# A depthwise convolution on TensorE: the first convolution's matmuls cut from 32x64 to 32x32 array tiles

## The reference

```
h = x.transpose(0, 2, 1)
h = conv1d_grouped(h, conv1_w, conv1_b, c)     # 256 groups: 1 channel -> 4 hidden, 5 taps, padding 2
h = gelu(h)
h = conv1d_grouped(h, conv2_w, conv2_b, c)     # 256 groups: 4 hidden -> 1 channel, 5 taps
h = layernorm(h.transpose(0, 2, 1) + x, ln0_g, ln0_b)
```

## Time and profile before

| what | value |
|---|---|
| median of 3 runs | 1867.98 us (1865.91 to 1868.26) |
| the profiled execution | 1865.91 us |
| its span, first to last instruction | 1864.1 us |
| mean granted TensorE clock | 0.997 of full |
| busy: PE, PEld, DVE, ACT, POOL | 99%, 82%, 76%, 50%, 54% of the span |
| busy in 18.84 to 58.00 us: PE, DVE, ACT, POOL | 39.16, 20.01, 21.70, 11.85 of 39.16 us |
| the 32 steps of the convolutions | 5.7 us to 153.4 us |

### The profile page before, as it was taken

How to read it: one execution, slowest core, us unless ns; L and a number is a source line. 1 busy time by engine, 2 the same in 40 slices (tenths; PEclk the granted TensorE clock), 3 DMA queues, 4 the chain that set the end, 5 groups by cost and what they waited for, 6 DMA issues and landing times.

```text
span 1864.1 us, 47990 instructions
## 1 busy us (share of the span) xinstructions
PE 1837.3 (99%) x20164; PEld 1527.0 (82%) x20164; DVE 1417.9 (76%) x3329; ACT 933.9 (50%) x1741; POOL 1010.7 (54%) x775
## 2 busy tenths in 40 slices
PE   8999999999999999999999999999999999999998
PEld 2335888888888888888887899999999999999998
DVE  3667788888888888888887757777777777777777
ACT  4554766677666766677666742222222222323221
POOL 1557998999989998999884012121212122222221
PEclk9999999999999999999999999999999999999999
DMA  8273210000102210000106831010101010101000
GB/s 305 116 267 119 92 59 2 14 25 2 36 2 104 92 36 2 26 12 2 59 2 213 283 97 46 24 39 30 35 35 35 33 36 24 46 23 46 23 12 24
DMA packets 25240, 115.49 MB, mean 62 GB/s; under 512 B 4480, under 2 KB 5440, under 8 KB 19904
## 3 DMA queue, kind: packets, MB, share of 16 engines
q1 hardware_dynamic: 21104, 89.69, 13.7%
q0 software_dynamic: 1152, 12.58, 1.9%
q10 hardware_dynamic: 2768, 10.15, 1.4%
HBM read 80.95 MB, written 31.46 MB: 60 GB/s over the span
## 4 chain that ended last, share of the span: by engine, by line
PE 95%; DVE 2%; ACT 1%; POOL 1%; issue 1%; DMA 0%; SPq 0%; ACTq 0%; DVEq 0%; POOLq 0%
PE bankC L33 13%; PE bankC L34 13%; PE bankC L32 13%; PE ring L32 7%; PE ring L34 6%; PE ring L33 6%; PE big L917 5%; PE big L34 3%; PE big L33 3%; PE big L32 3%; PE ring L854 3%; PE big L834 3%; PE hid_ps L242 3%; PE conv_ps L253 3%; PE ring L891 2%; PE ring L876 2%
## 5 line engine op out<-in xcount | busy, mean ns | idle before, releaser
L32 PE MATMUL bankC<-down_hi,act_hi 128*128 128x256 f32 x1024 | 290.4, 284 | 0.0
L33 PE MATMUL bankC<-down_lo,act_hi 128*128 128x256 f32 x1024 | 290.0, 283 | 0.0
L34 PE MATMUL bankC<-down_hi,act_lo 128*128 128x256 f32 x1024 | 289.6, 283 | 0.0
L1553 DVE TENSOR_TENSOR act_lo<-gel,act_hi 128x512 fp32r<-128x512 f32 x256 | 210.5, 822 | 8.8
L32 PE MATMUL bankC<-aT_hi,up_hi 128*128 128x512 f32 x512 | 202.2, 395 | 0.0
L34 PE MATMUL bankC<-aT_hi,up_lo 128*128 128x512 f32 x512 | 202.2, 395 | 0.0
L33 PE MATMUL bankC<-aT_lo,up_hi 128*128 128x512 f32 x512 | 202.1, 395 | 0.0
L1507 POOL TENSOR_TENSOR hC<-hC,vecC 128x1024 f32<-128x1024 f32 x16 | 38.7, 2419 | 291.3 <-PE turn L1406 291.3
L32 PEld LDWEIGHTS bankC<-down_hi,act_hi 128*128 128x128 f32 x1024 | 193.5, 189 | 1.4
L33 PEld LDWEIGHTS bankC<-down_lo,act_hi 128*128 128x128 f32 x1024 | 192.6, 188 | 1.4
L1513 POOL TENSOR_TENSOR rstdC<-var_epsC,minus_halfC 128x4 f32<-128x4 f32 x47 | 52.5, 1118 | 260.1 <-DVE var_epsC L1578 260.1
(11 more groups left out here) (205 smaller groups left out, 5241.3 us busy)
## 6 DMA issues: line engine op xcount, KB each, us to landing
raw_late<-in_AB SPq DMA_DIRECT2D x30, 320.0 KB, 3.7
u<-hA SPq DMA_DIRECT2D x8, 1024.0 KB, 5.0
u_next<-u SPq DMA_DIRECT2D x8, 1024.0 KB, 4.8
hC<-u SPq DMA_DIRECT2D x16, 512.0 KB, 4.0
xC<-in_x SPq DMA_DIRECT2D x16, 512.0 KB, 4.9
out<-w_flat SPq DMA_DIRECT2D x15, 512.0 KB, 2.6
w_flat<-in_AB SPq DMA_DIRECT2D x22, 320.0 KB, 3.8
w_split<-w_parts ACTq DMA_DIRECT2D x4, 1536.0 KB, 5.1
```

The costliest lines, as they stand in the source:

```text
L32: e.matmul(out, wh, xh, start=start, stop=False)
L33: e.matmul(out, wh, xl, start=False, stop=False)
L34: return e.matmul(out, wl, xh, start=False, stop=stop)
L1553: e.tensor_tensor(a_lo[:, fb, :], g, a_hi[:, fb, :].bitcast(F32), ALU.subtract).then_inc(s_act_lo, 1)
```

## The change

In `conv1`, each matmul with a 32x64 stationary tile (two positions s) is replaced by two with 32x32 tiles (one position s each), so there are 32 calls per step instead of 16. The loop over `half` becomes a loop over s; the choice of k is the same for s = 0, 1 and for s = 2, 3 as it was for the two halves. For each output element the two products are added in the same order as before. The wait for a free bank stands ahead of each call as before (only the first for each bank has an effect), and the increment of `s_hid` sits on the last call of each bank.

```
-                    for half in range(2):
-                        k = 1 - second if half else second
+                    for s in range(S):
+                        k = second if s < 2 else 1 - second
                         for j in range(ROWS):
-                            r, rows = slice(32 * j, 32 * j + 32), slice(64 * half, 64 * half + 64)
-                            out = hid_of(n, j)[rows, :].rearrange("p (b g) -> p b g", b=2)
+                            r = slice(32 * j, 32 * j + 32)
+                            out = hid_of(n, j)[32 * s:32 * s + 32, :].rearrange("p (b g) -> p b g", b=2)
                             src = xs[l][r, cp, k:k + COLS].rearrange("p (b g) -> p b g", b=2)
-                            bands = band1[r, cp, k, 2 * half:2 * half + 2, :].rearrange("p s c -> p (s c)")
                             w.wait_ge(s_hidden, ROWS * n + j - HID + 1)
-                            m = e.matmul(out[:, :, second:], bands, src[:, :, second:], start=not second, stop=bool(second))
-                            if second and half:
+                            m = e.matmul(out[:, :, second:], band1[r, cp, k, s, :], src[:, :, second:], start=not second,
+                                         stop=bool(second))
+                            if second and s == S - 1:
                                 m.then_inc(s_hid, 1)
```

## The result

The changed kernel takes 1877.32 us (median of 6 runs, 1874.20 to 1878.01), the kernel before 1867.31 us (6 runs, 1864.01 to 1868.26). The ratio is 1.0055 with a 95% interval of 1.0043 to 1.0066: 10 us slower, where +1.0 us was forecast, a range of 1865.0 to 1874.0 us, and 0.76 on "within 0.2%". The profiled execution took 1879.74 us, its span is 1877.9 us.

A forecast was written before the change was run, and what follows sets the result against it. PE was taken to bound the convolution stage; -0.02 + 0.056 = +0.036 us per step over 31 steps gave +1.1 us, less 0.14 us swallowed by waits, net +1.0 us: 1869.0 us, range 1865.0 to 1874.0 us.

The forecast's parts named there:

- Streaming: In conv1, sixteen tiles run at once, so four waves of 0.43 us remain and streaming costs nothing more.
- column tiles take turns: Rival: in conv1 only eight of sixteen tiles run together, eight waves, about 1920 us; chance 0.10.
- First wave: conv1's first wave gets shorter because weight loads are 32 columns wide instead of 64: -0.02 us per step.
- Last wave: conv1's last wave shows 15 start gaps instead of 7, at 7 ns each: +0.056 us per step.
- Issue: In conv1, 32 more loads and matmuls per step lie hidden under the 0.43 us waves, even at 10 ns a pair.
- The last paragraph of the prediction: Signs to check in the trace after, including PE idle ahead of the transposes; another costly wait had chance 0.03.
- The waits that swallow part of a delay: Two of PE's waits for convT in the convolution stage absorb part of the loss: 0.14 us back.
- pairs further apart: Rival: conv1's load-and-matmul pairs start slower, 1870.5 us at 10 ns, 1878 us at 27 ns; chance 0.12.

The follow-up runs named there:

- e7_tiles8: The changed kernel with positions s = 2 and 3 left out of conv1 from step 2 on, leaving eight 32x32 tiles: 1865.36 us.
- e1_adjacent16: The changed kernel with conv1's calls reordered so that each tile's first and second pass follow one another: 1928.65 us.
- e4_split8_paired: The kernel before with each conv1 call cut in two by columns, a tile's two half calls side by side, each overwriting: 1881.42 us.
- e8_mixed: Half of the change on the kernel before: positions 0 and 1 stay 32x64 tiles, 2 and 3 become 32x32 tiles: 1931.30 us.
- e11_mixed_grouped: Same mixed 32x64 and 32x32 tiles in conv1, but both passes of the wide tiles ahead of those of the narrow: 1922.75 us.

## Why the prediction was wrong

- *Streaming: right.* Sixteen tiles share a wave, and a wave on time is 0.43 us long (62.78 to 63.21 us). The rival "column tiles take turns" is out. The Trainium skill's rule behind it, in "TensorE: Matmul & The Clock Gate", Part 3, The mechanism, that loads overlap with running matmuls only in another row group, does not hold with four column tiles in each row group either: all 32 loads for sixteen tiles are done 0.25 us after conv1's first, while the first matmuls, of 0.61 us each, still run.
- *First wave: right.* -0.02 us (0.45 us against 0.47 us); in e7_tiles8 the whole conv1 is 0.03 us shorter.
- *Last wave: right for itself, mis-sized in effect.* 7 ns a gap where nothing is held (+0.056 us), but 17 ns after the hold, 14 x 10 ns = 0.14 us more.
- *Issue: the step that failed.* "Sixteen load-and-matmul pairs at 7 ns are 0.11 us of a wave of 0.43 us, so they lie under it" looked at the pace only. It left out how far ahead of the running matmuls the engine takes records in. The runs showed 64 records; one pass over sixteen tiles fills them, so the second pass waits until the first call is complete, 0.18 us, and then comes at 17 ns a tile. conv1 of the kernel before has just 64 records, so pace and reach could not be told apart there; of the short matmuls of the earlier trace rows, each some 0.2 us long, only about twenty pairs (40 records) are under way at once. The last paragraph of the prediction named an idle place "which would mean that the doubled records hold the queue back", and gave such a wait 0.03. The hold is inside conv1 and not ahead of the transposes, and PE shows no idle time in it, since other tiles are still busy.
- *The sum in its place.* -0.03 (narrow loads) + 0.05 (eight more gaps) + 0.18 (hold until the first call is complete) + 0.14 (17 ns instead of 7) + 0.02 (the last wave starts 0.45 us after the third instead of 0.43 us, as after loads that come late) = +0.36 us, measured +0.37 us. Why the pace after the hold is 17 ns, no run shows.
- *The waits that swallow part of a delay: right in kind, larger.* 0.14 us was forecast because the loss per step was small; at 0.37 us per step both waits vanish, 0.77 us.
- *The rival "pairs further apart"* gave 1878 us at 27 ns a pair, nearly the measured time, but by luck, from a mechanism that is not there: the first two waves keep 7 ns, and e1_adjacent16 and e4_split8_paired change the time by order alone.

## What to carry to other kernels

When a kernel runs small tiles of the array side by side, count the records in program order between a tile's matmul and its next one, loads included and fp32 calls as four: here nothing was held with 32 records between them, seven of twelve tiles were late with 48, and with 64 every tile but the first waited until the oldest call was complete. Order the calls so that every tile has work within 64 records (in e1_adjacent16 half of them had none, and conv1 took 3.96 us) and each tile's next work lies well within them, 32 records away here, and prefer fewer, wider calls that fill the array. Keep tiles of one size together: each change cost 0.16 us, and a group that does not fill the array left the rest of it idle.

## What the runs showed of the hardware

- TensorE took records in program order to a depth of 64 from the oldest incomplete one (e1_adjacent16: record 65 in, record 66 held by record 2); a record counts until the end that the profile gives it (0.03 us before the next load), not until its streaming ends. It counts records and not calls: 32 bfloat16 calls of two records passed without a hold.
- Within that reach, matmuls of different tiles start out of program order: the first matmul of a later call precedes the second of an earlier one (in the kernel after sixteen first matmuls from 62.32 us, their second ones from 62.78 us).
- Independent tiles started 7 ns apart in fp32 and some 3 ns apart in bfloat16; in fp32 it was 13 ns where both passes of a tile follow one another, and 17 ns after a hold. The Trainium skill, in "TensorE: Matmul & The Clock Gate", Part 3, Measured speedup vs the span model, counts about 4 ns a tile; the fp32 runs here show 7 ns.
- A change of tile size inside a stream of fp32 calls cost 0.16 us (e8_mixed against e11_mixed_grouped).
